# Attention scores of wide units computed in two equal pieces, with sink keys behind every block of keys

## The chip, the cores and the metric

The kernel runs on one core of a Trainium2 chip. The metric is the device time of one execution in microseconds (us), lower is better. The engines are TensorE (PE: matmuls, with its weight loads listed apart as PEld), VectorE (DVE), ScalarE (ACT), GpSimd (POOL) and SyncE (SP, which only issues DMAs here).

## The reference, cut to what matters

One layer: a LayerNorm of x, then an attention branch s and a feed-forward branch g, and at the end `x + s * silu(g)`. Only the attention branch is touched. There are 4 sequences of 1024 tokens, 1024 channels, 16 query heads and 4 key heads of 64 channels each:

```
WINDOW, SINK = 512, 4
mask = (j <= i) & (j >= i - (WINDOW - 1))
mask = mask | (j < SINK)
mask = mask & ((i >= SINK) | (j <= i))
att = einsum(q, k) * (1 / sqrt(64)); att = where(mask, att, -inf)
y = softmax(att) @ v;   out = y @ Wo.T
```

A query sees the 512 keys up to itself and always the first four keys of its sequence, the sinks.

## The kernel before

Attention comes first (`attend`), the output projection, the gate and the last LayerNorm after it (`finish`). In attention a **unit** is one block of 128 queries (`qb`, 0 to 7) of one key head `g`, with its four query heads. There are 32 units in a sequence (`s` = 8 g + qb) and 128 in all, 16 for each value of qb. Keys lie in blocks of 128. A unit sees `blocks_of(qb)` = min(qb + 1, 5) blocks, so 1, 2, 3, 4, 5, 5, 5, 5 of them. For qb of 5 to 7 the first block has dropped out of the window and its four sink keys are added (`has_sink`).

Scores need three products of a high and a low part (q_hi k_hi, q_hi k_lo, q_lo k_hi) summed in PSUM. The four heads are done as two **pairs**; the two heads of a pair use the two halves of the 128 rows of TensorE, 64 channels each, and write to two PSUM tensors `s_ps` of two banks (512 columns) each. In this document a **round** is one of the three products for both heads of a pair: two weight loads of q (64 x 128) and two matmuls over the same keys. One pair up to 512 keys takes three rounds. A unit with five blocks takes six: three over its first four blocks (512 columns), three over the last block (128 columns, or 132 with the sinks, which stand behind the block in `k_hi` and `k_lo`; those tiles have room for 132 columns in every block, but POOL fills in the four sink columns only for blocks 5 to 7, in `k_sinks`, L651).

Then, per head: DVE adds the mask, takes the row's maximum and stores to `probs` (`mask_scores`, L1277), ACT takes the exponential with its sum (L759), DVE divides (L1294), PE transposes the blocks of 128 (L1030), ACT copies them to `pt` (L750), and PE multiplies by v (L1066).

The order of the work on each engine is written out by hand. One step of the loop (`step`, L1102) on PE is: scores of pair 0 of this unit; two of the transposed blocks of the unit before; a projection or part of one, or the transposition of x for the next sequence; a tile of the feed-forward weights (L849); scores of pair 1; more transposed blocks; more projection; the product with v of the unit before. Scores of a pair wait for DVE to have masked the pair before it (`masked`), since both use the same `s_ps`.

Of the kernel before, what the change touches and what calls it, by code (L numbers as in the profile page):

```python
# [34 lines left out]
WB = WINDOW // P  # L35
WIDE = (WB + 1) * P
NEG = -3.0e38
# [128 lines left out]
def attend(nc, shared, WT, Y, BC, XS, x, gate_w, Wq, Wk, Wv, in_gamma, in_beta, agg_w, agg_b, pn_gamma, pn_beta, d1_w, d1_b, d2_w, d2_b,  # L166
           bc_w, bc_b):

    with ExitStack() as ctx:
# [13 lines left out]
        x_hi, x_lo, w = shared  # L183
        k_hi = sb("k_hi", [P, K_TILES, TB, P + SINK], F32R)
        k_lo = sb("k_lo", [P, K_TILES, TB, P + SINK], F32R)

# [210 lines left out]
        def stores_before(t):  # L397

            return t // 2 + 1 if t < K0 else t - K0

        def turned_in(b, s):


            if b == 0 and s in LATER:
                return "w", LATER[s]
            if b + 1 < B and 0 <= s - TURN0 < TB:
                return "x", b + 1, s - TURN0
            return None
# [24 lines left out]
        with nc.Block() as block:  # L433
# [162 lines left out]
            def _(pool):  # L596
# [9 lines left out]
                def build_masks():  # L606
                    pool.memset(mask[:, :], 0.0)
                    pool.memset(mask4[:, :], 0.0).then_inc(masks_ready, 1)
                    pool.wait_ge(masks_ready, 1)
                    for m in (mask, mask4):  # L610
                        pool.affine_select(out=m[:, 0:P], in_=m[:, 0:P], compare_op=ALU.is_ge, fill=NEG,
                                           base=-1, pattern=[[1, P]], channel_multiplier=-1)
                        pool.affine_select(out=m[:, WB * P:WIDE], in_=m[:, WB * P:WIDE], compare_op=ALU.is_ge, fill=NEG,
                                           base=0, pattern=[[-1, P]], channel_multiplier=1).then_inc(masks_ready, 1)
# [36 lines left out]
                def k_sinks(b, m):  # L651

                    pool.wait_ge(j_taken, NUMBER["k", b, 2 * m] + 1)
                    for k in (k_hi, k_lo):
                        for block_no in range(WB + 1, TB):
                            last = pool.tensor_copy(k[:, m, block_no, P:P + SINK], k[:, m, 0, 0:SINK])
                    last.then_inc(k_sink_ready, 1)
# [43 lines left out]
            def _(act):  # L701
# [51 lines left out]
                def exponentials(b, s, head):  # L753
                    _, qb = unit_of(s)
                    u = UNITS * b + s
                    width = blocks_of(qb) * P + (SINK if has_sink(qb) else 0)
                    slot = GROUP * (u % 2) + head
                    act.wait_ge(masked, GROUP * u + head + 1)
                    act.activation(probs[:, slot, 0:width], probs[:, slot, 0:width], ACT.Exp,  # L759
                                   bias=neg_max[:, slot:slot + 1], scale=-1.0,  # L760
                                   accum_out=row_sum[:, slot:slot + 1]).then_inc(exp_done, 1)
# [69 lines left out]
            def _(pe):  # L831
# [143 lines left out]
                def scores(b, s, pair):  # L975
# [10 lines left out]
                    if s % TB == 4 and g % 2 == 0 and pair == 0:  # L986
                        pe.wait_ge(j_taken, NUMBER["k", b, g + 1] + 1)
                    if s % TB == WB + 1 and g % 2 == 0 and pair == 0:
                        pe.wait_ge(k_sink_ready, 2 * b + g // 2 + 1)
                    if u or pair:  # L990
                        pe.wait_ge(masked, GROUP * u + 2 * pair)
                    first = qb - n + 1
                    pieces = [(0, slice(first, first + min(n, WB)), P)]
                    if n > WB:
                        pieces.append((BANK, slice(qb, qb + 1), P + (SINK if has_sink(qb) else 0)))
                    for o, blocks, keys in pieces:
                        width = (blocks.stop - blocks.start) * keys
                        for m, (qs, k) in enumerate(((q_hi, k_hi), (q_hi, k_lo), (q_lo, k_hi))):
                            for head in range(2):
                                h = slice(HS * head, HS * head + HS)  # L1000
                                last = pe.matmul(s_ps[head][:, o:o + width], qs[h, pair, bass.ts(qb, P)],  # L1001
                                                 k[h, g // 2, blocks, 0:keys], start=m == 0, stop=m == 2)
                    last.then_inc(scores_ready, 2)
# [8 lines left out]
                def turn_probs(u, i):  # L1012
# [16 lines left out]
                    for head in range(GROUP):  # L1029
                        last = pe.transpose(t_ps[(turns_before(u) + i) % 2][:, bass.ts(head, P)],  # L1030
                                            probs[:, GROUP * (u % 2) + head, P * i:P * i + P], ident[:, :])
                    last.then_inc(turned, 1)
# [146 lines left out]
            def _(dve):  # L1179
# [87 lines left out]
                def mask_scores(b, s, head):  # L1267
                    _, qb = unit_of(s)
                    u = UNITS * b + s
                    n = blocks_of(qb) * P  # L1270
                    width = n + (SINK if has_sink(qb) else 0)
                    m = mask4[:, 0:n] if qb == WB else mask[:, WIDE - n:WIDE - n + width]
                    slot = GROUP * (u % 2) + head
                    if u == 0 and head == 0:
                        dve.wait_ge(masks_ready, 4)
                    dve.wait_ge(scores_ready, GROUP * u + head + 1)
                    dve.tensor_tensor_reduce(out=probs[:, slot, 0:width], in0=s_ps[head % 2][:, 0:width], in1=m,  # L1277
                                             scale=-SCALE, scalar=-NEG, op0=ALU.add, op1=ALU.min,
# [8 lines left out]
                def divide(b, s, head):  # L1287
                    _, qb = unit_of(s)
                    u = UNITS * b + s
                    width = blocks_of(qb) * P + (SINK if has_sink(qb) else 0)  # L1290
                    slot = GROUP * (u % 2) + head
# [509 lines left out]
```

## Time and profile before

| | us |
|---|---|
| median of 3 runs (lowest, highest) | 2299.21 (2295.86, 2303.58) |
| the profiled execution's own time | 2301.23 |
| its span | 2299.5 |
| PE busy | 2216.2 (96%) |
| DVE busy | 1456.3 (63%) |
| ACT busy | 857.4 (37%) |
| POOL busy | 155.0 (7%) |

The mean granted clock of TensorE was 0.986 of its upper level, 2.4 GHz. Attention's steps lie between about 96 and 1570 us of the span; before them come the first transpositions and projections, behind them `finish`. In the timeline a row gives the start, the length, the engine, the line, the operation, the tiles written and read, the shape and how many instructions of one kind were merged. The length of a matmul row holds its way through the array too and overlaps the next row, so the pace of PE is read from start to start.

### The profile page before, as it was taken

The page shows a single profiled execution, that of the slowest core. Times are in us where ns is not written, and L with a number is a line of the kernel's source. Part 1 is how long each engine was busy: PE and PEld are TensorE (multiplying, and loading weights), DVE is VectorE, ACT ScalarE, POOL GpSimd, SP SyncE. Part 2 cuts the span into 40 slices and gives each one's busy share as a digit, 9 for nine tenths or more (in the row PEclk, how much of TensorE's full clock was granted, in tenths as well). Part 3 has the DMA queues.
Part 4 walks back from the last instruction along what each step waited for, and adds up shares of the span by engine and source line. Part 5 has one row for each costly group of instructions (what it writes and reads, how often), then busy time and mean ns, then how long its engine had stood idle before and what let it go on. Part 6 is the DMA issues. An engine that isn't in the chain of part 4 may idle for free. (4 is left out here: it accounts for less than half of the span.)

```text
span 2299.5 us, 35899 instructions
## 1 busy us (share of the span) xinstructions
PE 2216.2 (96%) x13577; PEld 1632.9 (71%) x13577; DVE 1456.3 (63%) x3071; ACT 857.4 (37%) x1837; POOL 155.0 (7%) x373
## 2 busy tenths in 40 slices
PE   6999999999999999999999999988999999999998
PEld 5766666767666676666676766656888888888886
DVE  6464666655666656556765556565667667667667
ACT  2254554435454434455443545454111111111111
POOL 2100001000001100000100000000100100101100
PEclk8999999999999999999999999999999999999999
DMA  7286448633546833444863353554342342432431
GB/s 270 91 273 190 144 153 282 208 102 121 165 161 197 259 136 125 158 131 148 276 216 99 123 206 130 213 189 155 122 146 94 143 139 99 146 129 108 146 116 67
DMA packets 173358, 366.53 MB, mean 159 GB/s; under 512 B 12425, under 2 KB 110857, under 8 KB 158881
## 3 DMA queue, kind: packets, MB, share of 16 engines
q1 hardware_dynamic: 167664, 346.21, 45.2%
q0 software_dynamic: 5120, 16.85, 2.1%
q8 instruction: 91, 1.49, 0.3%
q10 hardware_dynamic: 432, 1.57, 0.2%
q14 instruction: 51, 0.41, 0.1%
HBM read 284.79 MB, written 79.72 MB: 159 GB/s over the span
## 5 line engine op out<-in xcount | busy, mean ns | idle before, releaser
L750 ACT ACTIVATE pt<-t_ps 128x512 f32<-128x512 f32 x480 | 266.1, 595 | 538.3 <-PE t_ps L1030 536.5
L964 PE MATMUL j_ps<-x_hi,w 128*128 128x512 f32 x1232 | 414.9, 406 | 0.0
L759 ACT ACTIVATE probs<-probs,neg_max 128x644 f32<-128x644 f32 (+5 forms) x512 | 352.7, 694 | 60.0 <-DVE neg_max L1277 60.0
L1277 DVE CUSTOM_DVE_ANT_0 probs<-s_ps,mask 128x644 f32<-128x644 f32 (+5 forms) x512 | 316.5, 655 | 85.4 <-PE s_ps L1001 80.7
L1658 PE MATMUL out_ps<-wo,w 128*128 128x512 f32 x1536 | 353.5, 389 | 2.8 <-DVE w L1715 2.8
L1658 PEld LDWEIGHTS out_ps<-wo,w 128*128 128x128 f32 x1536 | 288.2, 188 | 63.0 <-issue 3.2
L1658 PE MATMUL gate_ps<-x_hi,w 128*128 128x512 f32 x1024 | 280.7, 391 | 5.6 <-POOL b_ident L1616 5.6
L1030 PE MATMUL t_ps<-ident,probs 128*128 128x128 f32 x1920 | 270.9, 280 | 10.7 <-ACT pt L750 4.7
L964 PEld LDWEIGHTS j_ps<-x_hi,w 128*128 128x128 f32 x1232 | 232.0, 190 | 53.7 <-issue 6.5
L1001 PEld LDWEIGHTS s_ps<-k_hi,q 64*128 64x128 f32 x1536 | 147.3, 186 | 172.4 <-issue 98.9
L1001 PE MATMUL s_ps<-k_hi,q 64*128 64x512 f32 (+4 forms) x1536 | 245.4, 353 | 10.0 <-DVE q L1249 5.6
L964 PE MATMUL j_ps<-x_lo,w 128*128 128x512 f32 x616 | 245.4, 398 | 0.0
L1030 PEld LDWEIGHTS t_ps<-ident,probs 128*128 128x128 f32 x1920 | 208.9, 141 | 51.3 <-issue 19.6
L1066 PE MATMUL o_ps<-pt,v 128*64 128x256 f32 x1920 | 236.9, 387 | 1.6 <-DVE small_rows L1209 1.5
L1658 PEld LDWEIGHTS gate_ps<-x_hi,w 128*128 128x128 f32 x1024 | 192.7, 189 | 46.0 <-POOL b_ident L1616 6.0
L1294 DVE TENSOR_SCALAR probs<-probs,inv_sum 128x644 f32<-128x644 f32 (+5 forms) x512 | 218.0, 468 | 9.1
L1066 PEld LDWEIGHTS o_ps<-pt,v 128*64 128x64 f32 x1920 | 127.2, 137 | 94.1 <-issue 42.4
L1643 ACT ACTIVATE b_res<-b_a 128x1024 f32<-128x1024 f32 x32 | 33.9, 1061 | 425.0 <-DVE b_a L1745 425.0
L1658 PE MATMUL gate_ps<-x_lo,w 128*128 128x512 f32 x512 | 158.1, 390 | 0.0
L849 PE MATMUL o_ps<-fw,cols 128*32 128x512 f32 x1088 | 142.9, 609 | 5.0 <-issue 2.8
L964 PEld LDWEIGHTS j_ps<-x_lo,w 128*128 128x128 f32 x616 | 117.5, 191 | 21.6
L1001 PE MATMUL s_ps<-k_lo,q 64*128 64x512 f32 (+4 forms) x768 | 129.6, 329 | 0.0
(180 smaller groups left out, 2197.5 us busy)
## 6 DMA issues: line engine op xcount, KB each, us to landing
fw<-in_L_ffn_d_w_dram SPq DMA_DIRECT2D x128, 1024.0 KB, 5.2
w<-WT SPq DMA_DIRECT2D x36, 1024.0 KB, 5.0
w<-XS SPq DMA_DIRECT2D x64, 512.0 KB, 6.3
XS<-x_hi SPq DMA_DIRECT2D x32, 512.0 KB, 7.9
XS<-x_lo SPq DMA_DIRECT2D x32, 512.0 KB, 9.4
Y<-y SPq DMA_DIRECT2D x256, 64.0 KB, 2.2
b_x<-in_L_attn_x_dram SPq DMA_DIRECT2D x32, 512.0 KB, 4.2
b_y<-Y SPq DMA_DIRECT2D x32, 512.0 KB, 6.5
```

The source lines that it names most:

```text
L750: act.activation(pt[:, m % PT_SLOTS, :, :], bank[:, :].rearrange("p (h q) -> p h q", q=P), ACT.Copy).then_inc(pt_ready, 1)
L759: act.activation(probs[:, slot, 0:width], probs[:, slot, 0:width], ACT.Exp, bias=neg_max[:, slot:slot + 1], scale=-1.0, accum_out=row_sum[ ...
L849: last = pe.matmul(f_ps[COLS * j:COLS * j + COLS, :], cols[:, B * first[j]:B * first[j] + COLS], fw[n % 2][:, bass.ts(j, BANK)], start=sta ...
L964: last = pe.matmul(bank_of((kind, b, n)), w[:, slot, wp * C + c * P:wp * C + c * P + P], xs[:, c, bass.ts(ch, BANK)], start=i == 0, stop=i ...
L1001: last = pe.matmul(s_ps[head][:, o:o + width], qs[h, pair, bass.ts(qb, P)], k[h, g // 2, blocks, 0:keys], start=m == 0, stop=m == 2)
L1030: last = pe.transpose(t_ps[(turns_before(u) + i) % 2][:, bass.ts(head, P)], probs[:, GROUP * (u % 2) + head, P * i:P * i + P], ident[:, :])
L1066: last = pe.matmul(o_ps[HS * half:HS * half + HS, 0:2 * P], lhs, rhs[:, half::2, :], start=i == 0, stop=i == turns_of(qb) - 1)
L1277: dve.tensor_tensor_reduce(out=probs[:, slot, 0:width], in0=s_ps[head % 2][:, 0:width], in1=m, scale=-SCALE, scalar=-NEG, op0=ALU.add, op1 ...
L1294: dve.tensor_scalar(probs[:, slot, 0:width], probs[:, slot, 0:width], inv_sum[:, slot:slot + 1], None, ALU.mult).then_inc(normed, 1)
L1643: act.activation(res[:, :], a[:, :], ACT.Sigmoid).then_inc(sig2_ready, 1)
L1658: last = pe.matmul(out_[:, bass.ts(half, BANK)], lhs[:, c, :], rhs(c, half), start=(c == 0 and lhs is hi and rhs is w_hi), stop=(c == KB - ...
```

## The change

Every block of keys now stands with the four sink keys behind it, 132 columns (`PADDED`), for all eight blocks of `k_hi` and `k_lo`. The scores of a unit are taken over one unbroken stretch of these columns: 132 for each block, without the last four where the unit has no sinks to add. That is 128, 260, 392, 524, 656, 660, 660, 660 columns for qb of 0 to 7. Where a stretch has more than 512 columns it is cut into two equal parts, one for each PSUM bank: 2 x 262 (qb 3), 2 x 328 (qb 4), 2 x 330 (qb 5 to 7). The mask holds a large negative number over the four columns between two blocks. DVE reads the two parts from the two banks in one instruction, with one more dimension in its pattern, and writes them side by side; exponential and division run over the same number of columns. The transpositions take the 128 columns of a block out of 132. POOL fills the sink columns of all blocks with one instruction for each of `k_hi` and `k_lo` instead of three, and PE waits for them before the unit with qb 1 instead of qb 5.

```diff
-WIDE = (WB + 1) * P
+PADDED = P + 4
+WIDE = (WB + 1) * PADDED - 4
...
+        def width_of(qb):
+            return blocks_of(qb) * PADDED - (0 if has_sink(qb) else SINK)
...
                     for m in (mask, mask4):
+                        pool.memset(m[:, 0:WB * PADDED].rearrange("p (n c) -> p n c", c=PADDED)[:, :, P:PADDED], NEG)
...
                     for k in (k_hi, k_lo):
-                        for block_no in range(WB + 1, TB):
-                            last = pool.tensor_copy(k[:, m, block_no, P:P + SINK], k[:, m, 0, 0:SINK])
+                        last = pool.tensor_copy(k[:, m, :, P:PADDED],
+                                                k[:, m, 0, 0:SINK].unsqueeze(1).to_broadcast([P, TB, SINK]))
...
-                    if s % TB == WB + 1 and g % 2 == 0 and pair == 0:
+                    if s % TB == 1 and g % 2 == 0 and pair == 0:
                         pe.wait_ge(k_sink_ready, 2 * b + g // 2 + 1)
...
-                    first = qb - n + 1
-                    pieces = [(0, slice(first, first + min(n, WB)), P)]
-                    if n > WB:
-                        pieces.append((BANK, slice(qb, qb + 1), P + (SINK if has_sink(qb) else 0)))
-                    for o, blocks, keys in pieces:
-                        width = (blocks.stop - blocks.start) * keys
+                    first, width = (qb - n + 1) * PADDED, width_of(qb)
+                    parts = 1 if width <= BANK else 2
+                    width //= parts
+                    for part in range(parts):
...
-                                last = pe.matmul(s_ps[head][:, o:o + width], qs[h, pair, bass.ts(qb, P)],
-                                                 k[h, g // 2, blocks, 0:keys], start=m == 0, stop=m == 2)
+                                last = pe.matmul(s_ps[head][:, BANK * part:BANK * part + width],
+                                                 qs[h, pair, bass.ts(qb, P)],
+                                                 k[h, g // 2, :, :].rearrange("p t c -> p (t c)")[
+                                                     :, first + width * part:first + width * part + width],
+                                                 start=m == 0, stop=m == 2)
...
-                    dve.tensor_tensor_reduce(out=probs[:, slot, 0:width], in0=s_ps[head % 2][:, 0:width], in1=m,
+                    dve.tensor_tensor_reduce(out=probs[:, slot, 0:width].rearrange("p (a n) -> p a n", a=parts),
+                                             in0=s_ps[head % 2][:, :].rearrange("p (a n) -> p a n", n=BANK)[
+                                                 :, 0:parts, 0:width // parts],
+                                             in1=m.rearrange("p (a n) -> p a n", a=parts),
```

On PE, in the first unit with sinks (qb 5 of the first key head), from the last product with v to the feed-forward tile; `t_ps` takes transposed blocks, `s_ps` the scores, and a count such as x2 is the two heads. Before:

```order
L1066 MATMUL o_ps<-pt,v 64x256 x8
L1001 MATMUL s_ps<-k_hi,q 128x512 x2
L1001 MATMUL s_ps<-k_lo,q 128x512 x2
L1001 MATMUL s_ps<-k_hi,q 128x512 x2
L1001 MATMUL s_ps<-k_hi,q 128x132 x2
L1001 MATMUL s_ps<-k_lo,q 128x132 x2
L1001 MATMUL s_ps<-k_hi,q 128x132 x2
L1030 MATMUL t_ps<-ident,probs 128x128 x8
L849 MATMUL o_ps<-fw,cols 32x512 x4
```

and now:

```order
L1075 MATMUL o_ps<-pt,v 64x256 x8
L1007 MATMUL s_ps<-k_hi,q 128x330 x2
L1007 MATMUL s_ps<-k_lo,q 128x330 x2
L1007 MATMUL s_ps<-k_hi,q 128x330 x4
L1007 MATMUL s_ps<-k_lo,q 128x330 x2
L1007 MATMUL s_ps<-k_hi,q 128x330 x2
L1039 MATMUL t_ps<-ident,probs 128x128 x8
L857 MATMUL o_ps<-fw,cols 32x512 x4
```

The number of matmuls is the same, six rounds, and what stands around them has not moved; the columns are 330 in every round.

On PE, in the unit with qb 3 of the first key head, pair 0. Before:

```order
L1066 MATMUL o_ps<-pt,v 64x256 x4
L1001 MATMUL s_ps<-k_hi,q 128x512 x2
L1001 MATMUL s_ps<-k_lo,q 128x512 x2
L1001 MATMUL s_ps<-k_hi,q 128x512 x2
L1030 MATMUL t_ps<-ident,probs 128x128 x8
```

and now:

```order
L1075 MATMUL o_ps<-pt,v 64x256 x4
L1007 MATMUL s_ps<-k_hi,q 128x262 x2
L1007 MATMUL s_ps<-k_lo,q 128x262 x2
L1007 MATMUL s_ps<-k_hi,q 128x262 x4
L1007 MATMUL s_ps<-k_lo,q 128x262 x2
L1007 MATMUL s_ps<-k_hi,q 128x262 x2
L1039 MATMUL t_ps<-ident,probs 128x128 x8
```

Three rounds of 512 columns have become six of 262, with twice the matmuls and weight loads.

## Rows read from the trace of the kernel before

**Rows 1.** Busy time by engine over attention's steps (PE, PEld, DVE, ACT, POOL), clock, DMA

```profile
96.00:1570.00 1474.00, 1431.22 (x10022) 986.47 (x10024) 906.21 (x2411) 716.74 (x1686) 66.02 (x180) 0.99 0.53 172
```

**Rows 2.** Groups by form: matmuls of scores over the last block with sinks

```profile
L1001 PE MATMUL s_ps<-k_hi,q 64*128 64x132 f32 x384 | 43.0, 246 | 0.0
```

**Rows 3.** Timeline of PE: pair 0 with five blocks and sinks, to pair 1

```profile
915.79 0.50 PE L1001 MATMUL s_ps<-k_hi,q 64*128 64x512 f32 x2
916.13 0.39 PE L1001 MATMUL s_ps<-k_lo,q 64*128 64x512 f32 x2
916.36 0.46 PE L1001 MATMUL s_ps<-k_hi,q 64*128 64x512 f32 x4
916.66 0.27 PE L1001 MATMUL s_ps<-k_lo,q 64*128 64x132 f32 x2
916.77 0.28 PE L1001 MATMUL s_ps<-k_hi,q 64*128 64x132 f32 x2
916.97 1.09 PE L1030 MATMUL t_ps<-ident,probs 128*128 128x128 f32 x8
...
918.99 0.50 PE L1001 MATMUL s_ps<-k_hi,q 64*128 64x512 f32 x2
```

**Rows 4.** Timeline of PE: pairs with three rounds of 128, 256, 384, 512 columns

```profile
943.80 0.33 PE L1001 MATMUL s_ps<-k_hi,q 64*128 64x128 f32 x2
943.97 0.28 PE L1001 MATMUL s_ps<-k_lo,q 64*128 64x128 f32 x2
944.08 0.27 PE L1001 MATMUL s_ps<-k_hi,q 64*128 64x128 f32 x2
944.28 1.10 PE L1030 MATMUL t_ps<-ident,probs 128*128 128x128 f32 x8
...
954.28 0.39 PE L1001 MATMUL s_ps<-k_hi,q 64*128 64x256 f32 x2
954.50 0.28 PE L1001 MATMUL s_ps<-k_lo,q 64*128 64x256 f32 x2
954.62 0.28 PE L1001 MATMUL s_ps<-k_hi,q 64*128 64x256 f32 x2
954.83 0.66 PE L1030 MATMUL t_ps<-ident,probs 128*128 128x128 f32 x4
...
960.95 0.44 PE L1001 MATMUL s_ps<-k_hi,q 64*128 64x384 f32 x2
961.23 0.34 PE L1001 MATMUL s_ps<-k_lo,q 64*128 64x384 f32 x2
961.40 0.33 PE L1001 MATMUL s_ps<-k_hi,q 64*128 64x384 f32 x2
961.67 1.09 PE L1030 MATMUL t_ps<-ident,probs 128*128 128x128 f32 x8
...
969.14 0.50 PE L1001 MATMUL s_ps<-k_hi,q 64*128 64x512 f32 x2
969.72 0.39 PE L1001 MATMUL s_ps<-k_hi,q 64*128 64x512 f32 x2
970.04 1.09 PE L1030 MATMUL t_ps<-ident,probs 128*128 128x128 f32 x8
```

**Rows 5.** Timeline of DVE: second mask operation beside the pair of rows 3

```profile
917.84 0.82 DVE L1277 CUSTOM_DVE_ANT_0 probs<-s_ps,mask 128x644 f32<-128x644 f32 x1
918.59 0.08 DVE L1277 DVE_READ_ACCUMULATOR2_ANT neg_max<- 128x1 f32 x1
```

**Rows 6.** Groups by form: the operations over a head's 644 columns

```profile
L759 ACT ACTIVATE probs<-probs,neg_max 128x644 f32<-128x644 f32 x192 | 158.8, 832 | 1.7 <-DVE neg_max L1277 1.7
L1277 DVE CUSTOM_DVE_ANT_0 probs<-s_ps,mask 128x644 f32<-128x644 f32 x192 | 151.3, 825 | 46.2 <-PE s_ps L1001 45.7
L1294 DVE TENSOR_SCALAR probs<-probs,inv_sum 128x644 f32<-128x644 f32 x192 | 98.0, 553 | 3.4
```

**Rows 7.** Timeline of POOL: sink keys of the second sequence, first two key heads

```profile
399.33 0.43 POOL L656 CAST k_hi<-k_hi 128x4 fp32r<-128x4 f32 x3 [1.60 <-DVE k_lo L1249]
```

More of the change, by code:

```diff
@@ L183, in attend @@
         x_hi, x_lo, w = shared
-        k_hi = sb("k_hi", [P, K_TILES, TB, P + SINK], F32R)
-        k_lo = sb("k_lo", [P, K_TILES, TB, P + SINK], F32R)
+        k_hi = sb("k_hi", [P, K_TILES, TB, PADDED], F32R)
+        k_lo = sb("k_lo", [P, K_TILES, TB, PADDED], F32R)
         v = sb("v", [P, 3, TB, 2, HS])
@@ L610, in build_masks @@
                     for m in (mask, mask4):
+                        pool.memset(m[:, 0:WB * PADDED].rearrange("p (n c) -> p n c", c=PADDED)[:, :, P:PADDED], NEG)
                         pool.affine_select(out=m[:, 0:P], in_=m[:, 0:P], compare_op=ALU.is_ge, fill=NEG,
                                            base=-1, pattern=[[1, P]], channel_multiplier=-1)
-                        pool.affine_select(out=m[:, WB * P:WIDE], in_=m[:, WB * P:WIDE], compare_op=ALU.is_ge, fill=NEG,
+                        pool.affine_select(out=m[:, WB * PADDED:WIDE], in_=m[:, WB * PADDED:WIDE], compare_op=ALU.is_ge, fill=NEG,
                                            base=0, pattern=[[-1, P]], channel_multiplier=1).then_inc(masks_ready, 1)
@@ L755, in exponentials @@
                     u = UNITS * b + s
-                    width = blocks_of(qb) * P + (SINK if has_sink(qb) else 0)
+                    width = width_of(qb)
                     slot = GROUP * (u % 2) + head
@@ L1030, in turn_probs @@
                         last = pe.transpose(t_ps[(turns_before(u) + i) % 2][:, bass.ts(head, P)],
-                                            probs[:, GROUP * (u % 2) + head, P * i:P * i + P], ident[:, :])
+                                            probs[:, GROUP * (u % 2) + head, PADDED * i:PADDED * i + P], ident[:, :])
                     last.then_inc(turned, 1)
@@ L1269, in mask_scores @@
                     u = UNITS * b + s
-                    n = blocks_of(qb) * P
-                    width = n + (SINK if has_sink(qb) else 0)
-                    m = mask4[:, 0:n] if qb == WB else mask[:, WIDE - n:WIDE - n + width]
+                    width = width_of(qb)
+                    parts = 1 if width <= BANK else 2
+                    m = mask4[:, 0:width] if qb == WB else mask[:, WIDE - blocks_of(qb) * PADDED + SINK:][:, 0:width]
                     slot = GROUP * (u % 2) + head
@@ L1289, in divide @@
                     u = UNITS * b + s
-                    width = blocks_of(qb) * P + (SINK if has_sink(qb) else 0)
+                    width = width_of(qb)
                     slot = GROUP * (u % 2) + head
```

## The prediction

> **What bounds the kernel now.** I read the shares of the engines first: PE is busy 96% of the span, and over the steps of attention 1431 of 1474 us, against 906 of DVE and 717 of ACT, at a granted clock of 0.99 of 2.4 GHz [rows 1]. So what counts is PE's pace, start to start. The timeline of PE shows it for a pair with five blocks and sinks [rows 3]: the pair starts at 915.79, the transpositions behind it at 916.97, 1.18 us in all. The rounds of 512 columns are 0.23 apart (916.13 to 916.36), but the two last rounds of 132 columns are 0.11 apart and not the 0.055 that 132 columns take at 2.4 GHz. Pairs with 128 columns show the same 0.11 [rows 4] (943.97 to 944.08): a round cannot be shorter than this, since it has two weight loads to do as well. The three rounds over the last block are therefore cheap in work and dear in time, and the change trades them for rounds that are long enough.
>
> **The pace of a round by its columns.** Rows 4 give, from the first start of a pair to the next kind of operation: 0.48 us for three rounds of 128, 0.55 for 256, 0.72 for 384, 0.90 for 512. Inside, one round is 0.11 at 128, 0.12 at 256 (954.50 to 954.62), 0.17 at 384 (961.23 to 961.40) and 0.23 at 512. What is left of a pair's time is about 0.20 (0.72 - 3 x 0.173, 0.90 - 3 x 0.233), spent where PE goes over from and to work on all 128 rows. Between 256 and 384 columns a round grows by about 0.05 us for 128 columns. No row has 330 columns: the nearest rows bound the round by 0.12 (256) and 0.17 (384), and on the line between them 330 lies at 0.15 and 262 at 0.12. I take these.
>
> **PE, part by part.**
> - Five blocks (qb 4 to 7; 64 units, 128 pairs, of which 96 have the sinks, as the 384 matmuls of 132 columns on k_hi say, four for a pair [rows 2]). Now 1.18, then 6 x 0.15 + 0.20 = 1.10, so 0.08 less, times 128: 10.2 us less. The bounds of a round put it between 6 x 0.12 + 0.20 = 0.92 (33 us less) and 6 x 0.173 + 0.20 = 1.24 (8 us more).
> - Four blocks (qb 3; 16 units, 32 pairs). They had 512 columns in three rounds and get 524, so they are cut too: now 0.90, then 6 x 0.12 + 0.20 = 0.92 to 0.93. 32 x 0.03 is 1.0 us more. At the floor of 0.11 it would be 0.86 (1 us less), at the 0.17 of 384 columns 1.24 (11 us more).
> - Two and three blocks (64 pairs) get 4 and 8 more columns in each of three rounds; at 0.05 us for 128 columns that is 5 to 10 ns a pair, 0.5 us more.
> - Transpositions, products with v and everything else on PE keep their number and place.
>
> Sum on PE: -10.2 + 1.0 + 0.5 = -8.7 us.
>
> **DVE and ACT.** A head with five blocks gets 16 columns more. Mask, exponential and division of 644 columns take 825, 832 and 553 ns [rows 6]; at most in proportion, 16 columns cost 21, 21 and 14 ns. Over all units (4, 8, 12 or 16 columns a head) it comes to some 7 us of DVE's and ACT's masking and exponentials, spread over engines that are idle 38% and 51% of that stretch [rows 1]. What is queued behind a mask operation is the next head's, and PE waits for both before pair 1. In rows 5 the second one ends its maximum at 918.67, and pair 1 starts at 918.99 [rows 3] after transpositions and a feed-forward tile; the slack is 0.32 us, and two longer masks take 0.04 of it. Pair 0 itself ends 0.08 earlier, which moves both alike. So I cost it at nothing, with 0.2 us for places where PE is waiting for ACT's copies. If the slack were gone, each ns more per mask would cost 2 ns in each of 64 units.
>
> The mask now reads two stretches in two banks. The trace has no such read. Below, an excess could not be a gain beyond the few ns of a start, since the operation's pace is one column in about 1.2 ns whatever its shape; above, the bound is the mask done as two operations, 0.08 us more for a second read of the maximum [rows 5] and under 0.2 us for a start, still inside 0.32 for the first head and 0.2 beyond it for both: up to 64 x 0.2 = 13 us. I take zero, since the same number of elements flows and the instructions are as many as before.
>
> **POOL.** Six copies of 128x4 become two of 128x32; three of them took 0.43 us [rows 7]. Two fills are added to the masks. The fastest end is nothing saved that matters, the slowest some tenths of a us each, on an engine that is busy 66 of 1474 us [rows 1]. PE's wait for the sinks moves from unit qb 5 to qb 1. The sink keys of the second sequence are written at 399.3 us [rows 7], right behind the key projection in step 27 of the sequence before, six steps ahead of the new wait. Nothing.
>
> **The sum.** 2301.2 us of the profiled execution, less 8.7, plus 0.2: 2292.7. The median of the runs shown is 2.0 lower than that execution: 2290.7, or 0.37% faster. About 0.3% (7 us) is what a measurement of this kernel tells from no change, so this lies just beyond it.
>
> **A rule weighed.** A round of two matmuls takes 0.23 us at 512 columns and 0.11 at 128 [rows 3, 4]. The Trainium skill ("TensorE: Matmul & The Clock Gate", section "Back-to-back issue gap") gives for a stream of weight loads and matmuls some 131 ns a matmul at 512 columns and 81 at 128, so that a matmul has a large part that does not depend on its columns. By that rule twelve matmuls of 330 columns would take as long as six of 512 and six of 128, and the units with qb 3 would lose some 0.4 us a pair, in all an estimated 14 us slower. The rows at 256 and 384 columns disagree with a straight line through such a part; what it would be by rows is the third rival below.
>
> **The rivals.**
> 1. *The round is shorter than the line says.* If the 0.015 us that a round of 512 or 384 has over its columns at 2.4 GHz went away in rounds of one unbroken stretch of keys, a round would be 0.14 at 330 and 0.11 at 262. A pair: 1.04 and 0.87, so -17.9 - 1.0 + 0.5 = -18.4: 2281. For it: before, the matmuls step over the four columns between blocks, and now they don't. Against: the excess is about the same at 256 columns (0.12 against 0.107), with one such step, as at 512 (0.23 against 0.213), with three [rows 4], so the steps don't make it.
> 2. *Part of the gain is taken back by a wait.* Where PE next waits for something that does not move with it (ACT's copies, the exponentials of heads 2 and 3, which got longer), the 0.08 us are used up there. If two thirds go, -3: 2296. For it: DVE and ACT pass each unit through in turn. Against: the slack of 0.32 us in rows 3 and 5, and PE idle only 3% of the stretch.
> 3. *A fixed cost for each round, slower.* One mechanism: time goes by rounds more than by columns. A straight line through 0.11 at 128 and 0.23 at 512 gives 0.175 at 330 and 0.153 at 262. Pairs of five blocks: 6 x 0.175 + 0.20 = 1.25 (+0.07, 9 us), pairs of qb 3: 1.12 (+0.22, 7 us), with the 0.5: 16.5 us slower, 2316. It decides from 0.163 us at 330 columns on. Against it: 0.12 and 0.17 at 256 and 384 columns are below that line.
> 4. *The mask on two stretches is dear.* If it took 0.41 us more (half as much again), pair 1 would come 2 x 0.41 - 0.32 = 0.5 us later in 64 units, 32 us, less 8.7: 2322. It decides from 0.16 us an operation on.
>
> **How the numbers follow.** The forecast has 0.60, with 2286 to 2296 as its own range (a round of 0.145 to 0.155, a spread of 2 us in the medians); rival 1 has 0.10, rival 2 0.20, rival 3 0.06, rival 4 0.04. Faster by over 0.3%: 0.8 of the forecast's 0.60 (where the round is at most 0.151) and rival 1, 0.58. Within 0.3%: 0.12 of the forecast and rival 2, 0.32. Slower: rivals 3 and 4, 0.10. The range goes from rival 1 at 2281 to the no change of 2299 and leaves the slower two out.
>
> **What the profile would show.** Right: starts of rounds 0.15 us apart at 330 columns and 0.12 at 262, a pair of five blocks 1.10 us long, a pair of qb 3 0.93, PE's busy time some 9 us less and its clock the same, the mask over 660 columns at 840 to 850 ns, pair 1 not released by DVE. The sum is wrong if a round of 330 columns is over 0.16 us, if PE's idle time in attention grows by more than 3 us, if the mask takes over 1 us, or if PE is seen to wait for POOL's sink keys at the second unit of a sequence.

## The result and the profile after

The changed kernel takes 2295.16 us (2292.27 to 2299.67, 17 runs), the kernel before on the same chip 2299.97 (2294.67 to 2303.58, 17 runs). The ratio is 0.9983 with a 95% interval of 0.9976 to 0.9991: 3.9 us less, between 2.1 and 5.5. The two medians lie 4.8 us apart; the 3.9 come from the ratio. The forecast was 8.7 us less on TensorE and 2290.7, 8.5 below the median it was given, so the direction is right and the size is less than half of it. The profiled execution took 2298.40 us with a span of 2296.6.

The page's line of busy times, and the row over attention that answers to [rows 1]:

```profile
PE 2210.1 (96%) x13769; PEld 1635.8 (71%) x13769; DVE 1465.1 (64%) x3071; ACT 859.6 (37%) x1837; POOL 152.0 (7%) x343
```

```profile
96.00:1570.00 1474.00, 1425.27 (x10230) 988.68 (x10230) 915.43 (x2411) 721.42 (x1686) 63.28 (x153) 0.99 0.54 172
```

PE is 6.1 us less busy, DVE 8.8 and ACT 2.2 us more, at about the same mean clock (0.989, before 0.986). The pair of [rows 3] on PE:

```profile
902.58 0.42 PE L1007 MATMUL s_ps<-k_hi,q 64*128 64x330 f32 x2
902.84 0.32 PE L1007 MATMUL s_ps<-k_lo,q 64*128 64x330 f32 x2
902.99 0.46 PE L1007 MATMUL s_ps<-k_hi,q 64*128 64x330 f32 x4
903.29 0.31 PE L1007 MATMUL s_ps<-k_lo,q 64*128 64x330 f32 x2
903.44 0.31 PE L1007 MATMUL s_ps<-k_hi,q 64*128 64x330 f32 x2
903.69 1.09 PE L1039 MATMUL t_ps<-ident,probs 128*128 128x128 f32 x8
```

A round of 330 columns is 0.15 us (903.29 to 903.44), the pair 1.11 where it was 1.18. The pair with four blocks, against the last pair of [rows 4]:

```profile
966.90 0.39 PE L1007 MATMUL s_ps<-k_hi,q 64*128 64x262 f32 x2
967.12 0.29 PE L1007 MATMUL s_ps<-k_lo,q 64*128 64x262 f32 x2
967.25 0.40 PE L1007 MATMUL s_ps<-k_hi,q 64*128 64x262 f32 x4
967.49 0.28 PE L1007 MATMUL s_ps<-k_lo,q 64*128 64x262 f32 x2
967.60 0.28 PE L1007 MATMUL s_ps<-k_hi,q 64*128 64x262 f32 x2
967.82 0.44 PE L1039 MATMUL t_ps<-ident,probs 128*128 128x128 f32 x2
```

0.92 us in place of 0.90, rounds 0.11 to 0.12. The forms over a head's columns, in place of [rows 6], and POOL's copies in place of [rows 7]:

```profile
L767 ACT ACTIVATE probs<-probs,neg_max 128x660 f32<-128x660 f32 x192 | 161.4, 845 | 1.9 <-DVE neg_max L1286 1.9
L1286 DVE CUSTOM_DVE_ANT_0 probs<-s_ps,mask 128x660 f32<-128x660 f32 x192 | 154.5, 842 | 40.4 <-PE s_ps L1007 40.3
```

```profile
399.88 0.20 POOL L663 CAST k_hi<-k_hi 128x32 fp32r<-128x32 f32 x1 [1.61 <-DVE k_lo L1258]
400.02 0.21 POOL L663 CAST k_lo<-k_lo 128x32 fp32r<-128x32 f32 x1
```

The mask over two stretches takes 842 ns for 660 columns, after 825 for 644: 17 ns for 16 columns and nothing for the second bank. So every single price of the forecast is met within 0.02 us, and the sum is not.

**Where the rest is.** I took the start and the end of all 256 pairs in both traces. The 128 pairs with five blocks take 8.6 us less in all, the 32 with four blocks 0.9 more, those with two and three blocks 1.4 more, those with one 0.4 less: 6.6 us less. Such a length runs to the next instruction, so it also holds the wait that PE may have in front of the transpositions. One pair of five blocks took 1.93 us before (131.81 to 133.74) and one 1.96 after (129.31 to 131.27), both at the upper clock level; what follows them is

```profile
133.74 1.06 PE L1030 MATMUL t_ps<-ident,probs 128*128 128x128 f32 x8 [0.68 <-DVE w L1265]
131.27 1.06 PE L1039 MATMUL t_ps<-ident,probs 128*128 128x128 f32 x8 [0.79 <-DVE w L1274]
```

These waits sum to 5.4 us before and 6.5 after. Without them the pairs are 7.7 us shorter. Then the waits of PE for DVE, wherever they stand, first before and then after (total, times, longest):

```profile
PE o_ps L1066 <- DVE small_rows L1311: 5.0, 6, 0.8
PE t_ps L1030 <- DVE w L1265: 2.7, 4, 0.7
PE t_ps L1030 <- DVE probs L1294: 1.8, 3, 0.9
PE o_ps L849 <- DVE y L1301: 1.6, 2, 1.3
```

```profile
PE o_ps L1075 <- DVE small_rows L1323: 5.9, 6, 1.0
PE t_ps L1039 <- DVE w L1274: 3.2, 4, 0.8
PE t_ps L1039 <- DVE probs L1306: 2.5, 4, 0.9
PE o_ps L857 <- DVE y L1313: 1.8, 2, 1.4
```

All four have DVE as releaser, and together they grow by 2.3 us: PE is earlier and DVE, with 16 more columns in each head of a five-block unit, is not. These rows hold some 1.1 us that are in the pairs' 6.6 already, so the two may not be added up. All of PE's idle time in attention is 42.9 us before and 44.5 after; 7.7 less and 1.6 more make 6.1 less, beside the 6.4 by which attention as a whole (first scores to first gate matmul) is shorter, 1475.5 after 1481.9.

Two other things differ between the traces. In attention the clock stands at its lower level in other places: a wait of the same length is followed by it in one trace and not in the other. After, then before:

```profile
289.90 0.69 PE L1007 MATMUL s_ps<-k_hi,q 64*128 64x392 f32 x2 [1.68 <-DVE h_pre L1333]
290.39 0.53 PE L1007 MATMUL s_ps<-k_lo,q 64*128 64x392 f32 x2
290.72 0.53 PE L1007 MATMUL s_ps<-k_hi,q 64*128 64x392 f32 x2
291.17 0.79 PE L972 MATMUL j_ps<-x_hi,w 128*128 128x512 f32 x1
```

```profile
292.95 0.44 PE L1001 MATMUL s_ps<-k_hi,q 64*128 64x384 f32 x2 [1.67 <-DVE h_pre L1321]
293.23 0.34 PE L1001 MATMUL s_ps<-k_lo,q 64*128 64x384 f32 x2
293.40 0.34 PE L1001 MATMUL s_ps<-k_hi,q 64*128 64x384 f32 x2
293.68 0.50 PE L964 MATMUL j_ps<-x_hi,w 128*128 128x512 f32 x1
```

From the end of the wait to the product with v PE needs 6.96 us after (to 296.86) and 4.11 before (to 297.06): 2.85 us for one such place. The granted clock from 289 to 299 us was 0.66 of 2.4 GHz after, 1.00 before:

```profile
289.00:299.00 10.00, 9.10 (x42) 6.51 (x43) 4.16 (x15) 2.91 (x6) 0.00 (x0) 0.66 0.41 157
```

```profile
289.00:299.00 10.00, 8.03 (x52) 5.81 (x51) 5.02 (x16) 5.83 (x14) 0.59 (x1) 1.00 0.50 172
```

Other places went the other way: over the whole of attention PE is busy at the lower level for 30.1 us before and 29.9 after, so between these two traces the clock makes nothing of attention's difference. And the closing stage (first gate matmul to the end) is 4.7 us longer, 725.8 after 721.1. Its last wait of PE, before and after:

```profile
2279.79 11.17 PE L1658 MATMUL out_ps<-wo,w 128*128 128x512 f32 x48 [2.76 <-DVE w L1715]
```

```profile
2276.91 13.87 PE L1670 MATMUL out_ps<-wo,w 128*128 128x512 f32 x48 [6.81 <-DVE w L1727]
```

PE arrives some 7 us earlier, waits 4.05 us longer for DVE and then takes 2.7 us more for the same 48 matmuls, at a granted clock of 0.79 where it was 1.00. Those 2.7 us cost nothing, since it is DVE that ends the kernel. Its last operation, before and after:

```profile
2295.23 1.23 DVE L1754 TENSOR_TENSOR b_res<-b_a,b_x 128x1024 f32<-128x1024 f32 x1
2292.35 1.23 DVE L1766 TENSOR_TENSOR b_res<-b_a,b_x 128x1024 f32<-128x1024 f32 x1
```

It starts 15.67 us behind the same operation of the tile before it in both, and 2.9 us earlier after, which is the difference of the two spans. So what counts in the closing stage is how late DVE is. It needs as long for four tiles (87.1 us in the trace before) as PE (4 x 21.76 = 87.0). Its lag, from the start of PE's output projection to the start of DVE's multiplication by the SiLU (L1747), grew from 9.2 us in the first tile to 10.0 in the last but one before, and from 8.6 to 14.1 after.

### The profile page after: what moved, and what is told of

It reads as the page before. It is cut to its first block and busy times, and to the rows that moved or that the text cites. A ratio compares the mean times of both kernels' runs of the same rounds, so it can differ in the third digit from the quotient of the medians.

```text
span 2296.6 us, 36253 instructions
## 1 busy us (share of the span) xinstructions
PE 2210.1 (96%) x13769; PEld 1635.8 (71%) x13769; DVE 1465.1 (64%) x3071; ACT 859.6 (37%) x1837; POOL 152.0 (7%) x343
## 5 line engine op out<-in xcount | busy, mean ns | idle before, releaser
L767 ACT ACTIVATE probs<-probs,neg_max 128x660 f32<-128x660 f32 (+5 forms) x512 | 357.4, 703 | 60.7 <-DVE neg_max L1286 60.4
L1286 DVE CUSTOM_DVE_ANT_0 probs<-s_ps,mask 128x660 f32<-128x660 f32 (+5 forms) x512 | 322.4, 667 | 77.8 <-PE s_ps L1007 73.5
L1007 PEld LDWEIGHTS s_ps<-k_hi,q 64*128 64x128 f32 x1664 | 151.9, 186 | 159.2 <-issue 97.9
L1007 PE MATMUL s_ps<-k_hi,q 64*128 64x330 f32 (+5 forms) x1664 | 248.4, 334 | 10.2 <-DVE q L1258 5.7
L1306 DVE TENSOR_SCALAR probs<-probs,inv_sum 128x660 f32<-128x660 f32 (+5 forms) x512 | 220.9, 474 | 9.0
L1007 PE MATMUL s_ps<-k_lo,q 64*128 64x330 f32 (+5 forms) x832 | 129.9, 304 | 0.0
```

The source lines that it names most:

```text
L1007: last = pe.matmul(s_ps[head][:, BANK * part:BANK * part + width], qs[h, pair, bass.ts(qb, P)], k[h, g // 2, :, :].rearrange("p t c -> p ( ...
L1286: dve.tensor_tensor_reduce(out=probs[:, slot, 0:width].rearrange("p (a n) -> p a n", a=parts), in0=s_ps[head % 2][:, :].rearrange("p (a n) ...
L1306: dve.tensor_scalar(probs[:, slot, 0:width], probs[:, slot, 0:width], inv_sum[:, slot:slot + 1], None, ALU.mult).then_inc(normed, 1)
```

## The experiments

Times are medians on the chip, measured alongside the kernel before; "closing" and "attention" are the two lengths just defined, from the profiled execution. The theories in the expectations changed as they fell, so each is named by what it says.

**The two kernels again, and a closing stage with two buffers for `bc`.** The first two are copies; the other two load the row of weights `bc` once for a sequence, four tiles ahead, into one of two buffers, and have the stage's loop written out:

```diff
-        gate_bias, gamma, beta, bc = (sb(n, [P, C]) for n in ("gate_bias", "gamma", "beta", "bc"))
+        gate_bias, gamma, beta, bc0, bc1 = (sb(n, [P, C]) for n in ("gate_bias", "gamma", "beta", "bc", "bc1"))
...
-                        sp.wait_ge(mixed, after(GROUP * group))
+                    if group > 1:
+                        sp.wait_ge(mixed, after(TB * (group - 1)))
```

> The kernel before once more, for a second trace and as the measure of scatter. Both theories: a ratio of 1.000, within 0.1%. From its trace the time of attention and of the closing stage apart. Theory 1 (TensorE's saving of 6 to 7 us arrives at the end of attention in full, and the closing stage, where VectorE's chain trails TensorE, gives part of it back) expects here a closing stage within 1 us of the 721 us that the first trace shows (first gate matmul at 1578.4 to the end at 2299.5). Theory 2 (the saving never reaches the end of attention, since clock drops behind stalls in attention eat it) expects attention of the two kernels to be only 4 us apart once several traces are compared, and equal closing stages.

> The changed kernel once more, for a second trace. Both theories: 0.998 of the time before, as measured. Theory 1: from the first gate matmul to the end 723 to 726 us again (725.8 in the first trace), so 2 to 5 us more than before, with VectorE's lag behind TensorE growing over the closing stage. Theory 2: 721 us, the first trace's growth having been chance, and an attention stage only 4 us shorter.

> The kernel before with the closing stage written out for its 32 tiles and with two buffers for the broadcast rows bc, loaded once per sequence four tiles ahead, so that VectorE no longer waits for bc (10.8 us over 8 waits). Theory 1: its lag behind TensorE doesn't grow any more; 0 to 3 us faster than before (2296 to 2299). Theory 2: the same.

> The changed kernel with the same edit of the closing stage. Theory 1: what was given back there comes out, so that it is 6 to 7 us below before_bc2, near 0.996 to 0.997 of the time before (2290 to 2292). Theory 2: only 4 us below before_bc2, as the two kernels stand now.

Measured, beside 2299.66: 2299.38 (ratio 0.9991 to 1.0010), 2296.85 (0.9977 to 0.9995), 2300.60 (0.9990 to 1.0012) and 2296.39 (0.9983 to 1.0001). Attention 1479.5, 1469.9, 1482.1 and 1472.6; closing 722.7, 728.6, 720.7 and 725.3. The gain of attention and the loss behind it are both there again, and the second `bc` buffer doesn't remove the loss. So waiting for `bc` is not what keeps DVE late: in the closing stage of the first two traces DVE waits 10.8 and 14.9 us for it and 99.0 and 99.3 for x, and with two `bc` buffers 102.7 and 109.3 us for x. The copy of the changed kernel has an attention 5.6 us shorter than the first trace of the same program (1475.5), without the fallen clock at 290 us: where the clock falls differs from execution to execution, not only from kernel to kernel. This can be taken out by an estimate: at 1.2 in place of 2.4 GHz, half of the time in which PE is busy at the lower level counts as lost. Attention less this half is 1466.8, 1466.2 and 1467.1 us in the traces of before, copy_before and before_bc2, and 1460.5, 1461.5 and 1460.9 in those of the changed kernel, copy_after and after_bc2. At equal clock the change shortens attention by 5.7 us.

**Only the units with five blocks, and parts of the change on the kernel before.** narrow_old has the changed kernel's five-block units and unpadded blocks in three rounds for the others; before_split3 has the kernel before with the pairs of qb 3 cut into two parts; wide_dve has the kernel before with 16 masked columns more in mask, exponential and division of five-block units.

```diff
+            if qb < WB:
+                return blocks_of(qb) * P
```
```diff
+                    if n == WB:
+                        pieces = [(0, slice(first, first + 2), P), (2 * P, slice(first + 2, first + 4), P)]
```
```diff
-                    width = blocks_of(qb) * P + (SINK if has_sink(qb) else 0)
+                    width = blocks_of(qb) * P + (SINK if has_sink(qb) else 0) + (PAD if qb >= WB else 0)
```

> The changed kernel for units with five blocks only: units with one to four blocks go back to blocks of 128 columns, three rounds (512 columns in one piece for qb 3), masked from and to unpadded columns. PE has as many matmuls as before. Theory 3 (attention saves 8.5 us, and the closing stage loses 4 to 7 since the program is larger by 192 matmuls and loads, whose place in memory or fetching slows its DMAs) expects attention 9 to 10 us shorter than before, a closing stage of 721 to 723 us and VectorE's lag staying at 10, so 2289 to 2291. Theory 4 (the closing stage loses for another reason, which comes with the five-block units or a shorter attention) expects 725 to 728 us and a lag that grows to 13 or more again: 2294 to 2296.

> The kernel before with nothing but the units of four blocks (qb 3) cut: 2 x 256 columns in six rounds in place of 512 in three, 192 matmuls and weight loads more, in all as many as the changed kernel has. In attention it should cost 32 x 0.02 = 0.6 us. Theory 3: the closing stage takes 725 to 728 us, VectorE's lag grows to 13 to 17, and the time is 4 to 7 us above before (2303 to 2306). Theory 4: closing stage 721 to 723 us, time within 1 us of before.

> The kernel before, TensorE as it was, but mask, exponential and division of units with five blocks run over 16 masked columns more, as in the changed kernel (656 and 660; the 16 columns read what lies behind the scores). If VectorE's and ScalarE's added work is hidden, as the prediction had it, attention is as long as before (1480 to 1482 us) and the time within 1 us of before. If it takes gain back, some 4 to 8 us slower.

Measured beside 2298.12: 2293.53 (0.9973 to 0.9994), 2299.66 (0.9996 to 1.0014), 2299.89 (0.9998 to 1.0016). Attention took 1473.0, 1480.9 and 1481.7 us, the closing stage 721.9, 721.3 and 721.2. The whole gain is in the five-block units. Pairs of 2 x 256 columns took 0.90 to 0.91 us in the trace, so cutting costs next to nothing by itself. before_split3 has as many matmuls as the changed kernel and no longer closing stage, which speaks against the program's size as the cause; and narrow_old, with the five-block units as changed, has no longer closing stage either, so the loss does not come with them each time. In wide_dve PE waits 5.5 us for DVE's `small_rows`, between 5.0 and 5.9, but the four rows of waits shown above are 11.7 us in all, between 11.1 and 13.4: the 16 columns by themselves make 0.6 of the growth of 2.3. That the rest comes with PE's earlier arrival is what is left, not shown apart. In time the columns cost 1.8 us at the median, with an interval from -0.5 to 3.7.

**A third buffer for x in the closing stage.** `bc` has one buffer again, x is loaded three tiles ahead; narrow_x3 is narrow_old with it. This takes away what DVE waits for most in that stage, the landing of x.

```diff
-        xt = [sb(f"b_x{s}", [P, C]) for s in range(2)]
+        xt = [sb(f"b_x{s}", [P, C]) for s in range(3)]
...
-                    if follows(t, 2):
-                        sp.dma_start(xt[s][:, :], x_flat[bass.ds(P * (t + 2), P), :]).then_inc(x_loaded[s], 16)
+                    if follows(t, 3):
+                        sp.dma_start(xt[t % 3][:, :], x_flat[bass.ds(P * (t + 3), P), :]).then_inc(x_loaded[t % 3], 16)
```

> The kernel before with the closing stage written out and a third buffer for the rows of x there (loaded three tiles ahead; bc once per sequence). VectorE's wait of 3 us a tile for x is gone, so its chain takes some 18.7 us a tile against TensorE's 21.76. Theory 5 (in the closing stage VectorE's chain, with the landing of x inside it, runs within 0.3 us a tile of TensorE's pace, and it is there that the changed kernel loses) expects VectorE's lag behind TensorE to stay at 9 us or less to the end, and 1 to 4 us less than before: 2295 to 2298. Theory 6 (the closing stage is no part of it; the saving of attention is 8 us in profiled executions only) expects no difference that depends on the stage.

> The changed kernel with the same closing stage. Theory 5: closing stage as long as before_x3's within 1 us, lag 9 or less, so that the whole saving of attention arrives: 8 us below before_x3, 2287 to 2290, ratio to before 0.995 to 0.996. Theory 6: 4 us below before_x3.

> Both at once: only five-block units in two equal parts, narrow units as before, and the closing stage with the third buffer. Theory 5: about 1 us below after_x3, 2286 to 2289, 0.995 of before; the fastest of all. Theory 6: 2291 to 2293.

Beside 2298.22: 2298.97 (0.9989 to 1.0013), 2296.67 (0.9977 to 1.0001), 2291.46 (0.9963 to 0.9983). In the traces the closing stage is now the same in all three (721.4, 721.7, 721.9) and the last lag of DVE 6.51 us in all three: with two x buffers it is the wait for x, as its landing happens to fall, that lets DVE get later from tile to tile. Attention was 1479.4, 1475.4 and 1472.2. But the timings of the first two differ by 2.3 us in medians and 3.0 in means, not by the 8 that this theory wanted, and before_x3 is no faster than the kernel before. Part of this is the clock: the mean granted clock was 0.9889 in the executions of before_x3 and 0.9857 in those of after_x3, and over the 257 executions of all kernels here 0.001 more of it goes with 0.59 us less. With that taken out, an estimate, the two are 4.9 us apart (3.2 to 6.5); attention at equal clock is 5.4 apart in their traces (1465.8 and 1460.4). Beside the 3.9 of the change (2.1 to 5.5) this leaves room for a loss of a us or two in the closing stage, but does not show it. narrow_x3 is the fastest kernel of this study, 0.27% under the kernel before.

**Thirty small operations on POOL at the start of the changed kernel,** which move its code and its first microseconds:

```diff
+                for _ in range(30):
+                    pool.memset(probs[:, 7, 520 + _:521 + _], 0.0)
```

> The changed kernel with 30 one-column fills more on POOL at the very start, so that every engine's program has the size that before_split3's has, whose closing stage was normal. If the longer closing stage comes from the program's size and so its place in memory, it is 721 to 723 us here, lag 10, and the time 2290 to 2292. If it does not, closing stage 725 to 728 us, lag over 13, and 2295 to 2297 as before.

2294.76 beside 2298.22 (0.9966 to 0.9989), closing 723.8, attention 1475.8. It lies between the two lengths that were expected, 721 to 723 and 725 to 728, and settles nothing on why x lands later.

**Every product of the scores four times.** This multiplies what the rounds gain, and leaves the closing stage alone:

```diff
-                    for part in range(parts):
+                    for part in 4 * list(range(parts)):
```

(in the kernel before `for o, blocks, keys in 4 * pieces`).

> The kernel before with every product of the scores done four times into the same place, with the same result; nothing else differs. In one profiled execution it shows a pair of five blocks with sinks of 0.20 + 4 x 0.98 = 4.1 us in place of 1.18. It is the base for the changed kernel with the same repetition. Theory A (TensorE's pace is gained as forecast, and only the closing stage gives some of it back) and theory B (attention itself keeps only half of what TensorE gains) expect the same of this one: 128 pairs with 3 x 0.98, 32 with 3 x 0.70, 32 with 3 x 0.52, 32 with 3 x 0.35 and 32 with 3 x 0.33 us more, in all some 376 + 67 + 50 + 34 + 32 = 560 us more, about 2860 us.

> The changed kernel with every product of the scores done four times, to be compared with the kernel before with the same repetition. The closing stage is as in the changed kernel. Theory A (every round's gain and loss reaches the end of attention, and the closing stage gives back a fixed 2.5 to 5 us): four times the trace's differences for a pair, 4 x 0.07 x 128 = 36 less, 4 x 0.025 x 32 = 3 more, 2 more for pairs of two and three blocks, so 31 less through attention, and 26 to 29 us less at the end. Theory B (attention keeps about half of what TensorE gains, the rest goes into waits or into stretches at the lower clock level, in proportion): 15 us less or under. By the forecast's sum: 4 x 8.7 = 35 less. In the trace a pair of five blocks with sinks lasts 0.20 + 4 x 0.90 = 3.8 us.

2860.85 (4 runs) and 2811.17 (4 runs): 49.7 us less, where 26 to 29 or under 15 were expected. Both theories fall, on the other side. The timeline of PE in the kernel before with the repetition:

```profile
1186.06 0.39 PE L1001 MATMUL s_ps<-k_lo,q 64*128 64x512 f32 x2
1186.29 0.46 PE L1001 MATMUL s_ps<-k_hi,q 64*128 64x512 f32 x4
1186.59 0.27 PE L1001 MATMUL s_ps<-k_lo,q 64*128 64x128 f32 x2
1186.70 0.56 PE L1001 MATMUL s_ps<-k_hi,q 64*128 64x128 f32 x4
1187.09 0.40 PE L1001 MATMUL s_ps<-k_lo,q 64*128 64x512 f32 x2
1187.32 0.45 PE L1001 MATMUL s_ps<-k_hi,q 64*128 64x512 f32 x4
```

and in the changed one:

```profile
1181.67 0.46 PE L1007 MATMUL s_ps<-k_hi,q 64*128 64x330 f32 x4
1181.97 0.31 PE L1007 MATMUL s_ps<-k_lo,q 64*128 64x330 f32 x2
1182.12 0.46 PE L1007 MATMUL s_ps<-k_hi,q 64*128 64x330 f32 x4
1182.42 0.31 PE L1007 MATMUL s_ps<-k_lo,q 64*128 64x330 f32 x2
1182.57 0.46 PE L1007 MATMUL s_ps<-k_hi,q 64*128 64x330 f32 x4
```

One more pass over five blocks costs 1.03 us before (1186.06 to 1187.09) and 0.90 after (1181.67 to 1182.57), 0.13 less, not the 0.08 that I had reckoned for each pass from 1.18 - 0.20. In a single pass 0.05 of it disappears in the change to the transpositions. Pairs are 4.25 to 4.29 and 3.80 to 3.84 us long, those of qb 3 2.99 and 3.14. 128 x 0.45 less 32 x 0.15 less some 1.6 for the narrow ones is 51; the traces have attention 2041.9 and 1992.3 (49.6 less, and 51.2 less at equal clock by the estimate above) and closing 721.3 and 721.0. Here everything that PE gains in its rounds arrives in the time, and the changed kernel's closing stage with two x buffers is no longer. So neither DVE's columns nor the closing stage must cost anything. PE waits for DVE 14 us in attention in both kernels here (13.7 and 14.1), against 25.7 and 27.9 with scores done once: with PE this much slower, DVE is less often close behind.

**Only the narrow units four times** (`(4 if qb < 3 else 1) *` in the same place), five-block units as they are:

> The kernel before with the scores of units with one, two and three blocks (qb 0 to 2) done four times into the same place; units with four and five blocks as they were. It adds 32 pairs with 3 x 0.33, 32 with 3 x 0.35 and 32 with 3 x 0.52 us, 116 us in all, about 2415 us, and puts work where TensorE waits longest for VectorE (units of qb 0 and 2). Both theories expect the same of it; it is the base for the changed kernel with the same repetition.

> The changed kernel with the scores of units with qb 0 to 2 done four times, to be compared with the kernel before with the same repetition. The units that the change is about have their scores once, as in the changed kernel: pairs of five blocks 0.07 us shorter (128 of them, 9.0 us), pairs of qb 3 0.02 to 0.03 longer (0.8 us), pairs of two and three blocks some 1 us longer in all, sum -7 us on TensorE. Theory A (the pace reaches the end when the waits and the closing stage don't differ): 7 us less, 5 to 8. Theory B (about half of the gain is lost around the five-block units whatever stands between them): 3.5 us less, as with the third x buffer. If the closing stage is again 2.5 to 5 us longer than in the kernel before with the same repetition, the timings show 2 to 4.5 us less and the trace shows 7 less through attention.

2415.49 (2414.16 to 2418.93, 5 runs) and 2419.64 (2416.73 to 2421.25, 5 runs): the changed one is 4.2 us slower at the median; the two ranges overlap. Both theories fall once more. The pairs in the traces are 5.9 us less in all (five-block pairs 1.11 against 1.18). Attention is nevertheless 1.9 us longer (1592.4, 1590.5), and closing 3.8 longer (730.7, 726.9). The stretches of 12 us behind the wait for `q` at the head of the second, third and fourth sequence, in the kernel before with the repetition and then in the changed one (the column before the last two is the granted clock):

```profile
512.00:524.00 12.00, 12.00 (x109) 9.32 (x109) 4.41 (x17) 2.97 (x9) 2.06 (x4) 1.00 0.05 11
914.50:926.50 12.00, 12.00 (x96) 9.48 (x97) 3.63 (x13) 2.56 (x7) 0.50 (x1) 0.86 0.00 0
1317.40:1329.40 12.00, 12.00 (x109) 9.35 (x109) 4.41 (x17) 2.99 (x9) 2.06 (x4) 1.00 0.06 13
```

```profile
514.60:526.60 12.00, 12.00 (x95) 9.42 (x97) 3.63 (x13) 2.55 (x7) 0.47 (x1) 0.86 0.01 1
917.20:929.20 12.00, 11.99 (x95) 9.43 (x97) 3.63 (x13) 2.55 (x7) 0.43 (x1) 0.86 0.00 0
1319.80:1331.80 12.00, 11.97 (x93) 9.38 (x95) 3.63 (x13) 2.56 (x7) 0.39 (x1) 0.86 0.01 2
```

The wait is the same 1.41 us in all six. Behind it the clock fell in one of three cases before and in three of three after, and fell stretches hold 13 to 16 matmuls fewer. Over the whole of attention PE is busy at the lower level for 20.5 us before and 37.0 after, some 8 us lost by the estimate above; less this, attention is 6.5 us shorter (1573.8 after 1580.3). So the pace of the rounds is gained here too, and in these two traces the clock and the closing stage take back more than that. The other executions lean the same way, with a mean granted clock of 0.9876 before and 0.9852 after; at equal clock the difference of the means is 1.4 us, from -1.0 to 3.9, so that a slower kernel is not shown.

## Why the prediction missed, step by step

- *The pace of a round by its columns*: right. 0.15 at 330 and 0.12 at 262. This also excludes rival 3, whose line gave 0.175, and rival 1, whose round was 0.14. On the rule of the Trainium skill weighed there ("TensorE: Matmul & The Clock Gate", "Back-to-back issue gap"), the trace disagrees with its sustained figures: 131 ns a matmul at 512 columns and 81 at 128 would be an estimated 215 ns for a round of two at 330, the trace has 150. The same section's formula for a matmul alone, columns at 2.4 GHz and 2.5 ns, gives an estimated 140, 112 and 216 ns for a whole round of 330, 262 and 512, against 150, 120 and 230: the round, not the matmul, follows it here.
- *Five blocks, 128 x 0.08 = 10.2*: nearly right, mis-sized. The pair is 1.11 and not 1.10, and its sum over the trace 8.6 us less, 9.7 without the waits at its end. In four places such a pair took 1.93 us before (from 131.81, 158.05, 229.15 and 310.79) and 1.96 after: there its gain goes into PE's wait for DVE's `w`, 0.68 us before and 0.79 after.
- *Four blocks +1.0, two and three blocks +0.5*: 0.9 and 1.4. The narrow pairs grew by 0.01 each at full clock (0.55 to 0.56, 0.72 to 0.73), the rest is pairs at the lower level. All pairs together, without waits, come to 7.7 us less beside the forecast's 8.7.
- *DVE and ACT cost nothing, 0.2 us for waits*: this is the step in attention that failed. The slack of 0.32 us that I read between pair 0 and pair 1 does hold there (PE's wait for `neg_max` is 1.5 and 1.6 us in all). But I had looked at the unit's own chain alone. PE waits for DVE in other places, for `small_rows`, `w`, `probs` and `y`, 11.1 us before and 13.4 after, and its idle time in attention as a whole grew by 1.6 us in the first two traces and 2.4 in the copies, where the forecast had 0.2. This is rival 2 with another releaser, DVE and not ACT, and with about 2 us of the 5.7 that it put at stake. The mask's price was a little high (17 ns for 16 columns, not 21): the forms of 128 and 640 columns, 286 and 820 ns, give 1.04 ns a column, not 1.2.
- *That the rest of the kernel passes a gain through unchanged*: not written down as a step, but the sum rests on it. In four traces with the change, two x buffers and scores done once the closing stage took 723.8 to 728.6 us, in a fifth, narrow_old, 721.9, and in five of the kind of before 720.7 to 722.7. The runs with a third x buffer show that the lag grows through DVE's wait for x; those with repeated scores show that it does not belong to the change (before 726.9 with the narrow units repeated, after 721.0 with all repeated).
- *POOL and the moved wait*: right, no wait for the sink keys in the trace, and the copies take 0.20 and 0.21 us.

The balance of the two traces is: pairs without waits -7.7, PE's idle time +1.6, small things -0.3 (attention -6.4), closing +4.7, and an attention that starts 1.2 us later before: the span -2.9. Of the 8.7 us forecast, then, the rounds gave 7.7, and PE's waits took back 1.6 to 2.4, which leaves some 5.7, as attention has it at equal clock; the measured gain is 3.9 (2.1 to 5.5). The two steps that failed are the 0.2 us for waits and the closing stage put at nothing.

**What stays open.** Why x lands later in the closing stage of one kernel than of another was not found: neither `bc`, nor cutting the pairs of qb 3, nor the small operations at the start decides it. Why the clock falls behind one wait and not behind an equal one was not found either. Two executions of the same program differ in it. In the mean it does not take the gain: the mean granted clock is 0.9891 over the 17 executions of the changed kernel and 0.9892 over 103 of the kernel before. What lies between 5.7 and 3.9 us then falls to the closing stage by exclusion, which is argued and not shown: the traces have it longer by 4.7, 5.9 and 4.6 us, one execution each, more than the timings leave room for, and how long it is in an ordinary execution is not known.

## What to carry to other kernels

Price a round from rows on both sides of its size: that gave the pace within 0.01 us. Then ask, for every place in which the busiest engine waits now, whether the thing waited for gets earlier too; those waits are short and many, and took some 2 us of the 8 gained here. When the gain is some 0.3% of the kernel, repeat the changed work several times in both kernels as one experiment to measure it, take away the closing stage's wait as another, and compare a stage at equal clock, by PE's busy time at the lower level: the spans of single traces differed by -2.9, -5.7 (two `bc` buffers) and +6.2 us (narrow units repeated) for the same change.

## What the runs showed that I had not expected

- Attention at equal clock repeats within a us between traces whose plain lengths differ by 5.6 (1460.5 and 1461.5 for the changed kernel), while the timings scatter by 7 to 9 us.
- A round of 128 columns behind one of 512 is cheap, and the way back is dear: 0.30 us for the two (1186.29 to 1186.59) and 0.39 (1186.70 to 1187.09), where 0.11 and 0.23 add up to 0.34. Over a whole pass this nearly cancels (1.03 us against 3 x 0.23 + 3 x 0.11 = 1.02). In a single pass there is no way back, which fits the 0.05 us by which it was cheaper (0.98). Nor is 0.11 us the least that a round can take, as the prediction had it: behind one of 512 columns 0.07 is left for a round of 128.
- The same wait of 1.4 to 1.7 us was followed by the lower clock level in one execution and by the upper one in another, at 1.7 us (12 us at 0.86) to 2.9 us a time. That is about half of the change's effect for each place.
- A mask operation that reads two stretches in two PSUM banks costs no more than its columns (842 ns for 660, 825 for 644).
